# One 128-row chunk in 48 of the edge gather moved from GpSimd to SyncE and ScalarE, row by row, and a new order of the tile work

## The reference

```
h = feats * rsqrt(deg_out)
m = segment_sum(h[src], dst) * rsqrt(deg_in)
x = (m @ W_gc + b_gc) + (feats @ W_res + b_res)
logits = x @ Wg + bg                 # 64 experts, the best two by softmax
y = x + sum of the two experts' w2(gelu(w1 x)), gated, at most 1024 tokens an expert
y = batchnorm(y) over the nodes
out = layernorm(feats + y)
```

## Time and profile before

| | us |
|---|---|
| median of 3 runs | 2944.16 |
| the profiled execution | 2947.52 |
| its span | 2945.7 |
| busy: TensorE matmul | 2071.2 |
| busy: TensorE weight load | 1711.2 |
| busy: VectorE | 1234.2 |
| busy: ScalarE | 410.9 |
| busy: GpSimd | 1890.4 |
| edge stage: first gather issued | 209.87 |
| edge stage: last gather issued | 2167.84 |
| last group's sum | 2191.82 |

### The profile page before, as it was taken

One profiled execution on the slowest core, in us unless ns is written; L12 is line 12 of the kernel. 1 busy time (PEld: TensorE's weight loads), 2 busy tenths in 40 slices (PEclk: granted clock), 3 DMA queues, 4 the chain that ended last, 5 costly groups with the idle time before them and its releaser, 6 DMA issues.

```text
span 2945.7 us, 44174 instructions
## 1 busy us (share of the span) xinstructions
PE 2071.2 (70%) x10250; PEld 1711.2 (58%) x10251; DVE 1234.2 (42%) x3115; ACT 410.9 (14%) x1358; POOL 1890.4 (64%) x1970
## 2 busy tenths in 40 slices
PE   8956555666656666666667777767766899999660
PEld 7944444454444555555556566556555788889650
DVE  8971121122223423444445455545563322222367
ACT  3010000000000000001001111111112223323113
POOL 0017777777777777777777777777735767777500
PEclk6556868778888878888888899989997999999885
DMA  8033333333333333333333333333324556656532
GB/s 297 0 102 106 106 106 106 105 107 108 108 107 107 110 108 109 109 109 110 109 108 111 111 109 112 111 110 112 111 60 130 173 163 204 197 194 203 189 104 87
DMA packets 205085, 362.81 MB, mean 123 GB/s; under 512 B 43080, under 2 KB 125814, under 8 KB 204814
## 3 DMA queue, kind: packets, MB, share of 16 engines
q0 software_dynamic: 93648, 230.69, 26.9%
q1 hardware_dynamic: 104058, 123.31, 13.0%
q10 hardware_dynamic: 7108, 6.43, 0.6%
HBM read 327.91 MB, written 57.52 MB: 131 GB/s over the span
## 4 chain that ended last, share of the span: by engine, by line
POOL 40%; PE 25%; issue 19%; DVE 7%; DMA 4%; DVEq 3%; ACT 1%; PEld 1%; POOLq 1%; ACTq 0%; SPq 0%; PEldq 0%
POOL ring L460 20%; POOL stage L460 18%; PE bank L1276 6%; PE bank L1270 6%; PE bank L1156 5%; PE bank L1136 3%; PE bank L1197 2%; PE bank L1261 1%; DMA ring<-nodes,slots 1%; DMA stage<-y 1%; PE bank L1176 1%; DVE stage L749 1%; POOL y L495 1%; DVE acc L1054 1%; PEld bank L1345 1%
## 5 line engine op out<-in xcount | busy, mean ns | idle before, releaser
L460 POOL DMA_INDIRECT ring<-table,ring_idx x792 | 751.4, 949 | 242.1 <-issue 239.9
L460 POOL DMA_INDIRECT stage<-table,ring_idx x771 | 731.3, 949 | 234.9 <-issue 232.9
L1156 PE MATMUL bank<-ring,hot 128*128 128x257 f32 x1056 | 306.9, 454 | 159.9 <-DMA ring<-table,ring_idx 145.1
L1156 PE MATMUL bank<-stage 128*128 128x257 f32 x1030 | 304.2, 460 | 138.8 <-DMA stage<-table,ring_idx 130.7
L1156 PEld LDWEIGHTS bank<-ring,hot 128*128 128x128 f32 x1056 | 238.6, 232 | 222.0 <-issue 142.8
L1156 PEld LDWEIGHTS bank<-stage 128*128 128x128 f32 x1030 | 236.1, 235 | 201.3 <-issue 127.3
L945 DVE TENSOR_TENSOR acc<-acc,bank 128x257 f32 x196 | 82.9, 423 | 567.5 <-PE bank L1156 529.2
L1156 PE MATMUL bank<-ring,stage 128*128 128x257 f32 x528 | 167.8, 487 | 109.2 <-DMA ring<-table,ring_idx 82.7
L1270 PEld LDWEIGHTS bank<-ring,stage 128*128 128x128 f32 x1984 | 235.0, 195 | 10.1 <-issue 3.9
L1270 PE MATMUL bank<-ring,stage 128*128 128x128 f32 x1984 | 238.1, 279 | 2.5 <-DVE ring L1001 1.1
L495 POOL DMA_INDIRECT y<-ring,slots x192 | 195.5, 1018 | 65.9 <-issue 47.6
(11 more groups left out here) (230 smaller groups left out, 2564.0 us busy)
## 6 DMA issues: line engine op xcount, KB each, us to landing
stage<-in_L_gnn_w_dram SPq DMA_DIRECT2D x128, 512.0 KB, 4.0
ring<-table,ring_idx POOLq DMA_INDIRECT x792, 2.8
y<-zeros SPq DMA_DIRECT2D x49, 256.0 KB, 2.2
stage<-y SPq DMA_DIRECT2D x14, 896.0 KB, 7.1
stage<-table,ring_idx POOLq DMA_INDIRECT x771
stage<-in_L_gnn_b_dram SPq DMA_DIRECT2D x64, 128.0 KB
nodes<-yS ACTq DMA_DIRECT2D x49, 128.0 KB
xs<-in_x_dram SPq DMA_DIRECT2D x1, 6144.0 KB
```

Of the source, the lines that this page charges most:

```text
L460: pool.indirect_dma_start(out=ring(q)[:, j, 0:D], out_offset=None, in_=table[:, :], in_offset=bass.IndirectOffsetOnAxis(ap=ring_idx[:, q, ...
L1156: last = pe.matmul(bank[:, 0:D + 1], hots[:, j, :], ring(q)[:, j, :], start=j == 0, stop=j == n - 1)
```

## The change

**One chunk in 48.** In every full round the eighth chunk of the sixth group (`ROW_Q`) is no longer gathered by GpSimd. Its 128 rows are fetched by 128 single DMAs of one row of 1 KB each: 96 by SyncE into a buffer of its own (`row_buf`, two halves for two rounds), 32 by ScalarE straight into the ring slot, in four turns of eight after the tick of the round's first four groups. SyncE first loads the chunk's 128 source numbers into one partition, then loads 32 of them at a time into registers and issues 32 DMAs. After its fourth turn ScalarE waits for SyncE's rows and copies them into the ring. TensorE waits for both before the sixth group. SyncE may be two buffers ahead of the copy.

**New orders.** There are three one-hot buffers in place of two, and VectorE makes them two groups ahead. In `extras` the second tile's one-hot matrix comes first, then the one-hots of the group two ahead (`later`), then the sum. In TensorE's tick `slots` comes first, then the transposes, then `places`, and there is no wait for `nd_deg`. ScalarE copies `xS` before it waits for the tile's degree, and `mS` behind it.

```diff
-HOTS = 2
+HOTS = 3
+ROW_Q = RING - 1
+BLOCK = 32
+SP_ROWS = 96
+ACT_ROWS = 8
+ACT_TURNS = (P - SP_ROWS) // ACT_ROWS
...
+        row_list = rng[0:1, :, 0:P].bitcast(I32)
+        row_buf = sb("row_buf", [P, 2, D])
...
+        def row_of(eng, reg):
+
+            node = nc.s_assert_within(eng.snap(reg), 0, N - 1,
+                                      skip_runtime_bounds_check_because="the list of sources holds nodes")
+            return table[bass.ds(node, 1), :]
+
+        def pool_chunks(q, final):
+
+            if final:
+                return LASTJ if q == LASTQ - 1 else CPG
+            return CPG - 1 if q == ROW_Q else CPG
...
+            def list_rows(it, par):
+                at = it * (RING * CPG * P) + (ROW_Q * CPG + CPG - 1) * P
+                sp.dma_start(row_list[0:1, par, :], src[bass.ds(at, P)].rearrange("(o e) -> o e", o=1)).then_inc(listed, 16)
+
+            def fetch_rows(it, par):
+                sp.wait_ge(listed, it * 16 + 16)
+                sp.sem_inc(sp_starts, 1)
+                for b in range(SP_ROWS // BLOCK):
+                    sp.load(row_regs, row_list[0:1, par, b * BLOCK:(b + 1) * BLOCK])
+                    for r in range(BLOCK):
+                        home = row_buf[b * BLOCK + r:b * BLOCK + r + 1, par, :]
+                        sp.dma_start(home, row_of(sp, row_regs[r])).then_inc(sp_rows[b], 16)
+                for b in range(SP_ROWS // BLOCK):
+                    sp.wait_ge(sp_rows[b], it * (16 * BLOCK) + 16 * BLOCK)
+                sp.sem_inc(rows_there, 1)
+
+            sp.wait_ge(code_ready, 1)
+            sp.wait_ge(nb_done, 1)
+            list_rows(0, 0)
+            sp.wait_ge(table_first, 16)
+            sp.wait_ge(table_rest, 16 * (NB - 1))
+            fetch_rows(0, 0)
+            list_rows(1, 1)
+            fetch_rows(1, 1)
+            with sp.Fori(1, (STEPS - 1) // 2) as i:
+                for par in range(2):
+                    it = i * 2 + par
+                    sp.wait_ge(list_read, it - 1)
+                    list_rows(it, par)
+                    sp.wait_ge(rows_placed, it - 1)
+                    fetch_rows(it, par)
...
-                    for j in range(LASTJ if final and q == LASTQ - 1 else CPG):
+                    for j in range(pool_chunks(q, final)):
...
+                    act.activation(xS[:, :], xs[:, bass.ds(i, 1), :], ACT.Copy)
                     act.wait_ge(nd_deg, i + 1)
-                    act.activation(mS[:, :], acc[:, bass.ds(i, 1), 0:D], ACT.Copy)
-                    act.activation(xS[:, :], xs[:, bass.ds(i, 1), :], ACT.Copy).then_inc(nd_in, 1)
+                    act.activation(mS[:, :], acc[:, bass.ds(i, 1), 0:D], ACT.Copy).then_inc(nd_in, 1)
...
+            def fetch_rows(it, par, turn, first):
+                r0 = SP_ROWS + turn * ACT_ROWS
+                if turn == 0:
+                    if first:
+                        act.wait_ge(table_first, 16)
+                        act.wait_ge(table_rest, 16 * (NB - 1))
+                    else:
+                        act.wait_ge(acc_added, it * RING)
+                    act.wait_ge(listed, it * 16 + 16)
+                    act.sem_inc(act_starts, 1)
+                act.load(row_regs, row_list[0:1, bass.ds(par, 1), r0:r0 + ACT_ROWS])
+                for r in range(ACT_ROWS):
+                    act.dma_start(ring(ROW_Q)[r0 + r:r0 + r + 1, CPG - 1, 0:D], row_of(act, row_regs[r])).then_inc(act_rows, 16)
+                if turn == ACT_TURNS - 1:
+                    act.sem_inc(list_read, 1)
+
+            def place_rows(it, par):
+                act.wait_ge(rows_there, it + 1)
+                act.sem_inc(act_starts, 1)
+                act.activation(ring(ROW_Q)[0:SP_ROWS, CPG - 1, 0:D], row_buf[0:SP_ROWS, bass.ds(par, 1), :],
+                               ACT.Copy).then_inc(rows_placed, 1)
+
             def step(it, first):
+                par = 0 if first else nc.s_assert_within(act.snap(it & 1), 0, 1,
+                                                         skip_runtime_bounds_check_because="it is a parity")
+                    if q < ACT_TURNS:
+                        fetch_rows(it, par, q, first)
+                    if q == ACT_TURNS - 1:
+                        place_rows(it, par)
...
-                if not (first and q < HOTS):
-                    dve.wait_ge(group_mm, it * RING + (q - HOTS + 1))
+                if not first:
+                    dve.wait_ge(group_mm, it * RING + (q + 1))
...
+            def extras(g, c, later):
 
                 first_tile, last_tile = field(dve, c, 0), field(dve, c, 1)
+
+                def rows_of(t):
+                    dve.drain()
+                    dve.tensor_scalar(dstx[:, :], dstT[:, bass.ds(g * CPG, CPG)], neg_tile[:, bass.ds(t, 1)], None, ALU.add)
+                    dve.drain()
+                    dve.tensor_tensor(hotx[:, :, :], iota_ps.unsqueeze(1).to_broadcast([P, CPG, P]),
+                                      dstx[:, :].unsqueeze(2).to_broadcast([P, CPG, P]), ALU.is_equal).then_inc(hotx_ready, 1)
+
+                def sum_of(t):
+                    dve.reg_add(extra, extra, 1)
+                    n = dve.snap(extra, min_val=1, max_val=GROUPS * NT)
+                    dve.wait_ge(groupx_mm, n)
+                    dve.tensor_tensor(acc[:, bass.ds(t, 1), :], acc[:, bass.ds(t, 1), :], banks[2][:, 0:D + 1], ALU.add)
                 with dve.If(last_tile > first_tile):
+                    second = a_tile(first_tile + 1)
+                    rows_of(second)
+                    later()
+                    sum_of(second)
+                    with dve.If(last_tile > first_tile + 1):
+                        with dve.Fori(first_tile + 2, last_tile + 1) as tile:
+                            t = a_tile(tile)
+                            rows_of(t)
+                            sum_of(t)
+                with dve.Else():
+                    later()
                 return first_tile
...
+                    def later(ahead=q + HOTS - 1):
+                        if ahead < (LASTQ if final else RING):
+                            one_hots(it, ahead)
+                        elif not final:
+                            one_hots(it + 1, ahead - RING)
                     c = group_code(dve, g)
-                    first_tile = extras(g, c)
-                    dve.drain()
-                    dve.wait_ge(group_mm, g + 1)
+                    first_tile = extras(g, c, later)
+                    dve.drain()
+                    dve.wait_ge(group_mm, g + (1 + HOTS))
...
-                if i is not None:
-                    pe.wait_ge(nd_deg, i + 1)
-
-                def places(t):
-
-                    pe.wait_ge(nd_pick, t + (DEPTH + 1))
-                    pe.matmul(banks[2][:, 5 * EX:6 * EX], tri[:, :], picked[:, :], start=True, stop=False)
-                    pe.matmul(banks[2][:, 5 * EX:6 * EX], ones_b[:, :], taken[:, :], start=False, stop=True).then_inc(nd_rank, 1)
-                behind(2, places)
...
+                def places(t):
+
+                    pe.wait_ge(nd_pick, t + (DEPTH + 1))
+                    pe.matmul(banks[2][:, 5 * EX:6 * EX], tri[:, :], picked[:, :], start=True, stop=False)
+                    pe.matmul(banks[2][:, 5 * EX:6 * EX], ones_b[:, :], taken[:, :], start=False, stop=True).then_inc(nd_rank, 1)
+                behind(2, places)
...
-                    pe.wait_ge(gath[q], it * (16 * CPG) + 16 * n)
+                    pe.wait_ge(gath[q], it * (16 * pool_chunks(q, False)) + 16 * pool_chunks(q, final))
+                    if q == ROW_Q and not final:
+                        pe.wait_ge(rows_placed, it + 1)
+                        pe.wait_ge(act_rows, it * (16 * (P - SP_ROWS)) + 16 * (P - SP_ROWS))
```

More of the change, by code:

```diff
@@ L224, in graph_moe_kernel @@
         code_ready = sem("code_ready")
+        listed, list_read, sp_starts = sem("listed"), sem("list_read"), sem("sp_starts")
+        sp_rows = [sem(f"sp_rows{b}") for b in range(SP_ROWS // BLOCK)]
+        rows_there, rows_placed, act_rows = sem("rows_there"), sem("rows_placed"), sem("act_rows")
         idx_ready = sem("idx_ready")
@@ L384, in weights @@
                 sp.dma_start(b2s[:, par, :], b2[bass.ds(e, 1), :].rearrange("o d -> (o d)").partition_broadcast(P)).then_inc(b2_in[par], 16)
+            row_regs = [sp.alloc_register(f"sp_row{r}") for r in range(BLOCK)]
+            def list_rows(it, par):
[27 more added lines that the diff above has]
+                    fetch_rows(it, par)
             sp.wait_ge(slots_mm, 1)
@@ L619, in _ @@
             act.wait_ge(code_ready, 1)
+            row_regs = [act.alloc_register(f"act_row{r}") for r in range(ACT_ROWS)]
+            def fetch_rows(it, par, turn, first):
[18 more added lines that the diff above has]
+                               ACT.Copy).then_inc(rows_placed, 1)
             def step(it, first):
+                par = 0 if first else nc.s_assert_within(act.snap(it & 1), 0, 1,
```

(8 more changed lines are left out.)

28 lines of the change are left out of this document (7 added, 21 removed).

## The result

The changed kernel takes 2956.58 us (median of 8 runs), the kernel before 2945.43 us beside it. The ratio is 1.0047, 95% interval 1.0035 to 1.0059: slower by half a per cent, where 2901 us had been forecast. The profiled execution took 2967.8 us, 11 us above the median; times inside it are read with that in mind.

What follows compares the result with a forecast made beforehand. GpSimd's gathers were taken to bound the kernel, the other engines just keeping pace. Gathers -40.1, tail and orders -4, ScalarE +1 gave -43.1 us, from a median of 2944.2 to 2901 us; range 2888 to 2965.

Steps and rivals of the forecast that it cites:

- What is removed: GpSimd's gathers: one fewer in each of 32 full rounds, 1.2535 us each, 40.1 us saved, all on the path.
- SyncE: SyncE's 96 rows: 50.6 us a round, 51 to 55 if hindered, hidden behind GpSimd's 58.9 us at no cost.
- a load of some microseconds: SyncE's register loads: 0.5 us each assumed; taking some microseconds was named as a sign that the prediction is wrong.
- The pause that was put once into SyncE's two rounds: SyncE's long loop body: 4.4 us once in two rounds, counted as 2.2 us a round.
- That the others can follow: TensorE, VectorE and ScalarE behind the gathers: could follow nearly the whole gain, 39.6 us at 1800 us.
- ScalarE's 32 rows: ScalarE's four turns of 4.3 us and a copy, 17.6 us a round; cost 1 us for the whole stage.
- GpSimd's waits: Sign on GpSimd: waits for `acc_added` or indices summing to more than 10 us would show the prediction wrong.
- ScalarE delays the late ticks: Rival on ScalarE: a tile takes 22 instead of 19.6 us over the last 8 tiles, 19 us lost, 2920 us; chance 12%.
- The new orders: TensorE, VectorE and ScalarE orders: 2.3 us less per tile late on, some 4 us off the tail, bounds 0 to 8.
- the two waits of the earlier trace: TensorE late in the stage: 0.60 us for the next group's one-hots and 1.08 us for the second tile's, both to go.
- a slower GpSimd: Rival on the gathers: small DMA traffic lengthens each by 2%, 38 us eat the gain, 2939 us; chance 6%.
- SyncE's pace: Rival on SyncE: its round outlasts the gathers', slower from 60.5 us on, 2993 us at 62, 3057 at 64; chance 21%.

Runs made afterwards that it cites:

- e5_again: Changed kernel with ScalarE's turns ahead of the tile work and VectorE's one-hots back ahead of its code word load; ratio 0.9931 to the kernel before.
- e6_old_act_first: Kernel before plus the row fetches, with the old orders and ScalarE's turns and copy ahead of the tile work; ratio 0.9917.
- e10_104: Kernel before plus row fetches, old orders, turns ahead of tile work, SyncE 104 rows in register loads of 26, ScalarE three turns; ratio 1.0432.
- e7_supply: Kernel before with 32 gathers left out and their rows fetched in round 0 alone, old orders; output differs from the reference; ratio 0.9850.
- e12_no_turns: Kernel before plus row fetches, old orders, ScalarE's 32 rows fetched in round 0 alone, SyncE's rows and the copy kept; ratio 0.9878.
- e1_rows: Kernel before plus the row fetches alone, with its old orders, two one-hot buffers and waits, turns behind the tile work; ratio 1.0042.
- e2_again: Changed kernel without its row fetches: all 1563 gathers kept, new orders and third one-hot buffer only; ratio 1.0064 to the kernel before.

## Why the prediction was wrong

*What is removed* was right: 1531 gathers at 0.946 us, and where little holds them up the last starts at 2123.9 (e5_again) or 2128.5 (e6_old_act_first), forecast 2128.

*SyncE* was right in the sum and off in its terms. From row to row are 0.42 us in the changed kernel (25 DMAs start from 1227.9 to 1237.9), not 0.44; a load of 32 registers is 2.12 us, not 0.5, so that three of them take 6.4 us and not 1.5. In e6_old_act_first 12 list DMAs between 900 and 1600 us are (1559.9 - 915.6) / 11 = 58.6 us apart. Between 900 and 1800 us, 15.4 such rounds, SyncE waits 99.7 us for ScalarE, 6.5 a round. That leaves 52.1 us of work, forecast 50.6. The dearer loads and the cheaper rows and landings (1.4 us of waiting instead of 2.2) partly cancel, which is luck. The forecast had named a load of some microseconds as a sign against it; it came, and the round still hid under 58.9 us.
```profile
L411 SPq DMA_DIRECT2D rng<-in_src_dram x12: 224/228/230, 915.6 to 1559.9; - x12
```
```profile
SPq L411 <- ACTq L693: 99.7, 13, 18.6
```
The pause that was put once into SyncE's two rounds can be seen as well. In e10_104, where it never waits for ScalarE, its list DMAs at 1230.17, 1293.13, 1358.91, 1421.60 and 1486.95 us are in turn 62.7 to 63.0 and 65.4 to 65.8 us apart: some 2.7 us more in every second round, forecast 4.4. The pages of the profiles also count the packets of an instruction queue, here in e7_supply, e12_no_turns and e1_rows:
```profile
q14 instruction: 253, 2.07, 0.2%
q14 instruction: 344, 2.82, 0.3%
q14 instruction: 345, 2.83, 0.3%
```
SyncE's loop brings 91 more packets, ScalarE's turns one. With the rule that the prediction took from the Trainium skill, "Advanced Engine Details and Errata", section ISA Cache, SyncE's loop would reload and ScalarE's not; these counts agree with it.

*That the others can follow* was right: 35.0 of 40 us (e7_supply), 29 to 36 by other readings.

*ScalarE's 32 rows* is the step that failed, with its +1 us. The size of a turn was right: 3.8 to 4.1 us, forecast 4.3 (the load of 8 registers is 0.55 us and not 0.3, the rows are closer together, 8 in 3.26 us). That ScalarE would still have time for each tick's input was right too: TensorE waits for it (`mS`) 21.6 us in 15 ticks of the changed kernel from 1800 to 2200 us, and 31.7 in 22 of e2_again from 1600 to 2172 us, which fetches no rows: 1.4 us a tick in both. What the step left out is a reader of the turn's own product. It put two things behind a turn, the index write and the next tick's input, and not the rows, which TensorE needs for the sixth group. The fourth turn starts when ScalarE ends the fourth group's tick, and TensorE has only the fifth group to do in between. In the stretch above it had ended that group at 2088.27, before the turn began at 2088.83; then come 3.8 us of turn and the landing, to 2094.13. It waits up to 7.8 us, and the 16 matmuls behind such a wait take 5.2 to 6.7 us instead of 3.75. The forecast had named GpSimd's waits as a sign too, and they came: 30.5 us for the index writes, 9.9 for ring slots. All but about 1 us of the first falls after 1900 us, and the other engines end 54 us behind the last gather, about the five groups of slack that the step counted on; in e12_no_turns the same wait is 2.1 us. So it looks like a result of the waits for rows rather than a second cause, though no run shows it apart. The turns cost 48 us where they stand, and 0.0039 x 2947 = 11 us if they stand ahead of the tile work (e6_old_act_first against e12_no_turns; what these 11 us are stays open). The rival "ScalarE delays the late ticks" named the engine but not the mechanism, and priced it at 19 us.

*The new orders* were to bring 4 us. They cost 0.0064 x 2947 = 19 us alone (e2_again), 0.0005 x 2947 = 1.5 beside the rows as they are, and 0.0026 x 2947 = 8 with the turns ahead; where TensorE waits for rows anyway, most of their cost does not show; that it lies beside that wait is argued and not shown. The forecast struck out the two waits of the earlier trace rows because the wait for one-hots would go. It asked neither what the removed work had covered (the code word) nor where TensorE's idle time would gather. VectorE's pause at a round's start stayed as well: 4.2 to 5.1 us in the seven rounds from 1700 us on in the changed kernel, three times ahead of a second tile's one-hots.

The time above the forecast is 2956.6 - 2901 = 56 us. ScalarE's turns make 48 - 1 = 47 of it, the orders 4 + 1.5, and the supply 5 (35.0 instead of 40.1): 57.5. This is no independent check, since all but the supply's term are differences of the same ratios; the rough balance of TensorE's waits in e1_rows is the only one. That 2956.6 us still lies inside the stated range of 2888 to 2965 is luck: the range reached so far up for a slower GpSimd and for SyncE's pace, and neither was the cause.

## What to carry over

When DMA issues are given to an engine with idle time, ask for each of its products who reads it and when, the product of the new work first; then place the new work where the engine would idle for a producer, not behind it. A deeper buffer moves an engine's idle time rather than removing it; look at what comes right behind the place where it gathers.

## What the hardware showed

A register load took longer the more registers it filled: 0.30 us for 1 (TensorE), 0.55 for 8 (ScalarE), 2.12 for 32 (SyncE), whose blocks of words are 128 bytes apart. Loads of 26, whose blocks are 104 bytes apart, took in turn some 2.1 us (blocks at byte 0 and 208 of the list) and some 5.5 us (at 104 and 312); whether the place is the cause was not tested apart. A DMA of one row of 1 KB whose address is in a register keeps its queue 0.225 us, and is 0.42 us from start to start on SyncE, register work included. The gathers took 946 to 949 ns with them and without. A loop of two rounds cost SyncE some 2.7 us once in a pass, and VectorE stood 4.2 to 5.1 us idle at the start of its rounds. One chip ran the same program 30% longer, with a longest pause of VectorE of 18.0 us; there the new orders were a gain of 0.9%, and the kernels with rows as well took 13% longer than the kernel before.
